# An LSTM step on one core: the forget gate in PSUM banks of its own, its product with the cell apart, and the cell by one scan

## What is computed

```python
xW = einsum('ntd,dg->ntg', x, Wx) + b
def step(carry, xw_t):
    prev_h, prev_c = carry
    a = xw_t + prev_h @ Wh                 # (2, 1024): i, f, o, g of 256 each
    i = sigmoid(a[:, :H]);  f = sigmoid(a[:, H:2*H])
    o = sigmoid(a[:, 2*H:3*H]);  g = tanh(a[:, 3*H:])
    next_c = f * prev_c + i * g
    next_h = o * tanh(next_c)
    return (next_h, next_c), next_h
x = x + lstm(x, cond)
ys = cond / sqrt(256)
d = rsqrt(einsum('bi,io->bo', ys*ys, w*w) + 1e-8)
x = x + einsum('bsi,io->bso', x * ys[:, None, :], w) * d[:, None, :]
```

## Time and profile before

| | us |
|---|---|
| median of 3 runs (lowest to highest) | 1865.49 (1864.79 to 1865.72) |
| the profiled execution | 1865.51 |
| its span, first to last instruction | 1863.7 |
| PE busy / PEld busy | 1794.8 (96%) / 1627.1 (87%) |
| DVE busy | 916.5 (49%) |
| ACT busy | 900.9 (48%) |
| POOL busy | 259.2 (14%) |
| granted TensorE clock, mean | 0.994 |

### The profile page before, as it was taken

The page is one execution under the profiler, slowest core; times in us unless marked ns, Lnnn a source line. Parts: engine busy times, 40 slices in busy tenths (PEclk is TensorE's granted clock), DMA queues, the critical chain, the costliest instruction groups (busy, mean ns, idle before and its releaser), DMA issues.

```text
span 1863.7 us, 358217 instructions
## 1 busy us (share of the span) xinstructions
PE 1794.8 (96%) x165116; PEld 1627.1 (87%) x165116; DVE 916.5 (49%) x11034; ACT 900.9 (48%) x6148; POOL 259.2 (14%) x1293
## 2 busy tenths in 40 slices
PE   7999999999999999999999999999999999999998
PEld 6888888888888888888888888888888888888886
DVE  2454544455445544454444544455444544455444
ACT  2444444444444444444444444444444444444443
POOL 0111111111111111111111111111111111111110
PEclk7999999999999999999999999999999999999999
DMA  3000000000000000000000000000000000000001
GB/s 98 0 0 0 0 0 0 0 0 0 0 0 0 0 0 0 0 0 0 0 0 0 0 0 0 0 0 0 0 0 0 0 0 0 0 0 0 0 0 45
DMA packets 4585, 6.69 MB, mean 4 GB/s; under 512 B 1248, under 2 KB 3040, under 8 KB 4576
## 3 DMA queue, kind: packets, MB, share of 16 engines
q1 hardware_dynamic: 3872, 5.51, 0.9%
q10 hardware_dynamic: 704, 1.05, 0.2%
HBM read 4.46 MB, written 2.10 MB: 4 GB/s over the span
## 4 chain that ended last, share of the span: by engine, by line
PE 85%; DVE 10%; ACT 3%; issue 2%; DMA 0%; SPq 0%; POOL 0%; DVEq 0%
PE pG L209 51%; PE pX L191 17%; PE pS L209 12%; DVE junk L340 6%; PE pF L222 3%; ACT gates L176 3%; DVE hst L351 2%; DVE pG L322 1%; PE pX L290 1%; DVE gates L340 0%; DMA xh<-in_xT_dram 0%; PE pS L281 0%; DVE ores L368 0%; SPq L105 0%; ACT tanhc L182 0%
## 5 line engine op out<-in xcount | busy, mean ns | idle before, releaser
L209 PEld LDWEIGHTS pG<-hst,wh_sb 128*32 128x32 f32 x98304 | 981.1, 111 | 219.1 <-DVE hst L351 172.1
L209 PE MATMUL pG<-hst,wh_sb 128*32 128x16 f32 x98304 | 1081.8, 186 | 60.6 <-DVE hst L351 53.4
L340 DVE CUSTOM_DVE_ANT_1 junk<-gates 128x4 f32<-128x4 f32 x4096 | 506.9, 162 | 824.7 <-ACT gates L176 772.5
L176 ACT ACTIVATE gates<-pG 128x6 f32<-128x6 f32 x2048 | 372.5, 182 | 928.7 <-PE pG L209 782.9
L209 PE MATMUL pS<-hst,wh_sb 128*32 128x16 f32 x32768 | 495.5, 185 | 0.0
L191 PE MATMUL pX<-xp,wx_sb 128*32 128x8 f32 x32896 | 459.3, 181 | 2.8 <-issue 1.8
L137 POOL TENSOR_TENSOR xh<-xh,hst 128x4 f32 (+1 forms) x1024 | 208.6, 204 | 1575.4 <-DVE hst L351 1575.4
L182 ACT ACTIVATE tanhc<-gates 128x2 f32<-128x2 f32 x2048 | 410.5, 200 | 13.5
L209 PEld LDWEIGHTS pS<-hst,wh_sb 128*32 128x32 f32 x32768 | 397.9, 108 | 0.0
L191 PEld LDWEIGHTS pX<-xp,wx_sb 128*32 128x32 f32 x32896 | 391.8, 108 | 3.2 <-issue 1.9
L351 DVE TENSOR_TENSOR hst<-tanhc,ogate 128x2 f32<-128x2 f32 x2048 | 329.7, 161 | 100.4 <-ACT tanhc L182 0.2
(11 more groups left out here) (30 smaller groups left out, 13.9 us busy)
## 6 DMA issues: line engine op xcount, KB each, us to landing
outT_dram<-ores SPq DMA_DIRECT2D x8, 256.0 KB, 2.5
xh<-in_xT_dram SPq DMA_DIRECT2D x6, 320.0 KB
wh_sb<-in_Wh_dram ACTq DMA_DIRECT2D x1, 1024.0 KB, 8.0
wx_sb<-in_Wx_dram SPq DMA_DIRECT2D x1, 1024.0 KB, 7.4
w_sb<-in_w_dram SPq DMA_DIRECT2D x1, 256.0 KB, 6.9
xh<-in_xT_dram SPq DMA_DIRECT2D x2, 64.0 KB, 7.9
condT<-in_condT_dram ACTq DMA_DIRECT2D x1, 2.0 KB, 7.7
bias_col<-in_bC_dram ACTq DMA_DIRECT2D x1, 3.0 KB, 7.4
```

What stands on the lines that cost most here:

```text
L176: act.activation(gates[:, j, :, 0:NG].rearrange("p b n -> p n b"), cells[j][:, :, cols], ACT.Sigmoid).then_inc(gates_ready[j], 1)
L209: last = pe.matmul(to[c * Q:(c + 1) * Q, :], tile(wh_sb[:, k, :], c, j, g), hst[:, k, WIDE * t:WIDE * (t + 1)], start=False, stop=True, sk ...
L340: cell = dve.tensor_tensor_reduce(out=junk[:, j, b, :], in0=gates[:, j, b, AT_I:AT_F + 1].unsqueeze(2).broadcast_to([P, 2, 2]), in1=gates[ ...
```

## The change

It does five things:

1. The forget gate's sums move from `pG` to a PSUM tensor `pH`, one bank for each half; `pX` shrinks from three banks to one. `pG` keeps i and g (`pairs`).
2. On PE the order within a step changes: behind `h_ready[0]` come 12 matmuls of half 0 and 4 of half 1 (i alone), then the wait for `h_ready[1]`; behind it the forget gate of half 0 is finished first and signals `fsum_ready[0]`, then i and g signal `sums_ready[0]`; the same for half 1.
3. ACT takes sigmoid(f) alone (`fgate`), then i and g together into `parts`, for each half. DVE multiplies f by the cell (`tensor_tensor`) and writes the product into `parts`; when both writers have signalled `parts_ready[j]`, one `tensor_tensor_scan` over 6 elements gives the cell: for each batch row s; then 1*s - 0.5; then i*(s - 0.5) + f*c. It replaces the two `tensor_tensor_reduce`.
4. On ACT the tanh of half 0 stands ahead of the output gate of half 0; for half 1 the order stays (output gate, tanh). The signal for h (`factors_ready[j]`) comes from whichever is last.
5. The carries are split (`carry_pair`, `carry_forget`, `carry_outs`), and the filler of step 3 goes.

The core of the diff:

```diff
-    FILL = (0, 0, 1, 1)
+    FILL = (0, 0, 1, 0)
...
-        pX = ctx.enter_context(nc.psum_tensor("pX", [P, K + 1, 512], F32))
+        pH = ctx.enter_context(nc.psum_tensor("pH", [P, K, 512], F32))
+        pX = ctx.enter_context(nc.psum_tensor("pX", [P, 512], F32))
...
                     for j in range(K):
+                        act.wait_ge(fsum_ready[j], it * T + (s + 1))
+                        act.activation(fgate[:, j, :], forgets[j][:, cols], ACT.Sigmoid).then_inc(fgate_ready[j], 1)
                         act.wait_ge(sums_ready[j], it * T + (s + 1))
-                        act.activation(gates[:, j, :, 0:NG].rearrange("p b n -> p n b"), cells[j][:, :, cols],
-                                       ACT.Sigmoid).then_inc(gates_ready[j], 1)
-                    for j in range(K):
+                        act.activation(parts[:, j, SCAN - 1:SCAN - 1 + 8].rearrange("p (n q) -> p n q", n=2)[:, :, ::SCAN],
+                                       pairs[j][:, :, cols], ACT.Sigmoid).then_inc(parts_ready[j], 1)
+                    def cell_tanh(j):
+                        act.wait_ge(cell_ready[j], it * T + (s + 1))
+                        return act.activation(tanhc[:, j, :], cellc[:, j, SCAN - 1::SCAN], ACT.Tanh, scale=2.0)
+
+                    def out_gate(j):
                         act.wait_ge(osum_ready[j], it * T + (s + 1))
-                        act.activation(ogate[:, j, :], outs[j][:, cols], ACT.Sigmoid)
-                        act.wait_ge(cell_ready[j], it * T + (s + 1))
-                        act.activation(tanhc[:, j, :], gates[:, j, :, AT_C], ACT.Tanh, scale=2.0).then_inc(tanh_ready[j], 1)
+                        return act.activation(ogate[:, j, :], outs[j][:, cols], ACT.Sigmoid)
+
+                    cell_tanh(0)
+                    out_gate(0).then_inc(factors_ready[0], 1)
+                    out_gate(1)
+                    cell_tanh(1).then_inc(factors_ready[1], 1)
...
                     pe.wait_ge(h_ready[0], it * T + (s + 1))
-                    for n in range(NG):
-                        cell(s, 0, n, 0)
+                    cell(s, 0, 0, 0)
+                    cell(s, 0, 2, 0)
                     if s == 0:
-                        pe.wait_ge(x_carried[1], it + 1)
+                        pe.wait_ge(forget_carried[0], it + 1)
+                    cell(s, 0, 1, 0)
+                    if s == 0:
+                        pe.wait_ge(pair_carried[1], it + 1)
                     cell(s, 1, 0, 0)
-                    cell(s, 1, 1, 0, early)
 
                     pe.wait_ge(h_ready[1], it * T + (s + 1))
-                    for n in range(NG):
-                        last = cell(s, 0, n, 1)
-                    last.then_inc(sums_ready[0], 1)
-                    cell(s, 1, 1, 0, late)
+                    cell(s, 0, 1, 1).then_inc(fsum_ready[0], 1)
+                    cell(s, 0, 0, 1)
+                    cell(s, 0, 2, 1).then_inc(sums_ready[0], 1)
                     cell(s, 1, 2, 0)
-                    for n in range(NG):
-                        last = cell(s, 1, n, 1)
-                    last.then_inc(sums_ready[1], 1)
                     if s == 0:
-                        pe.wait_ge(x_carried[K], it + 1)
+                        pe.wait_ge(forget_carried[1], it + 1)
+                    cell(s, 1, 1, 0)
+                    cell(s, 1, 1, 1).then_inc(fsum_ready[1], 1)
+                    cell(s, 1, 0, 1)
+                    cell(s, 1, 2, 1).then_inc(sums_ready[1], 1)
+                    if s == 0:
+                        pe.wait_ge(outs_carried, it + 1)
...
                     for j in range(K):
-                        dve.wait_ge(gates_ready[j], it * T + (s + 1))
-                        for b in range(B):
-                            cell = dve.tensor_tensor_reduce(
-                                out=junk[:, j, b, :], in0=gates[:, j, b, AT_I:AT_F + 1].unsqueeze(2).broadcast_to([P, 2, 2]),
-                                in1=gates[:, j, b, AT_G:AT_G + 6].rearrange("p (a c) -> p a c", a=2)[:, :, ::2],
-                                scale=1.0, scalar=0.0, op0=ALU.mult, op1=ALU.add,
-                                accum_out=gates[:, j, b, AT_C:AT_C + 1])
-                        cell.then_inc(cell_ready[j], 1)
-                        if s == T - 1 and j == 0:
-                            carry_cells(0)
+                        dve.wait_ge(fgate_ready[j], it * T + (s + 1))
+                        dve.tensor_tensor(parts[:, j, (B + 1) * SCAN - 1::SCAN], fgate[:, j, :], cellc[:, j, SCAN - 1::SCAN],
+                                          ALU.mult).then_inc(parts_ready[j], 1)
+                        if s == T - 1 and j == 1:
+                            carry_pair(0)
+                        dve.wait_ge(parts_ready[j], it * (2 * T) + 2 * (s + 1))
+                        dve.tensor_tensor_scan(cellc[:, j, :], parts[:, j, 0:B * SCAN], parts[:, j, B * SCAN:2 * B * SCAN], 0.0,
+                                               ALU.mult, ALU.add).then_inc(cell_ready[j], 1)
                     for j in range(K):
-                        dve.wait_ge(tanh_ready[j], it * T + (s + 1))
+                        dve.wait_ge(factors_ready[j], it * T + (s + 1))
...
                         if s == T - 1 and j == 0:
-                            carry_cells(1)
+                            carry_forget(0)
+                            carry_pair(1)
                     if s == T - 1:
+                        carry_forget(1)
                         carry_outs()
```

More of the change, by code:

```diff
@@ L46, in build @@
         hst = sb("hst", [P, K, T * WIDE])
-        gates = sb("gates", [P, K, B, CELL])
-        junk = sb("junk", [P, K, B, G])
+        parts = sb("parts", [P, K, 2 * B * SCAN])
+        fgate = sb("fgate", [P, K, B])
+        cellc = sb("cellc", [P, K, B * SCAN])
         ogate = sb("ogate", [P, K, B])
@@ L81, in build @@
         osum_ready = [sem(f"osum_ready{j}") for j in range(K)]
-        gates_ready = [sem(f"gates_ready{j}") for j in range(K)]
+        fsum_ready = [sem(f"fsum_ready{j}") for j in range(K)]
+        fgate_ready = [sem(f"fgate_ready{j}") for j in range(K)]
+        parts_ready = [sem(f"parts_ready{j}") for j in range(K)]
         bias_doubled = sem("bias_doubled")
-        x_carried = [sem(f"x_carried{n}") for n in range(K + 1)]
+        pair_carried = [sem(f"pair_carried{j}") for j in range(K)]
+        forget_carried = [sem(f"forget_carried{j}") for j in range(K)]
+        outs_carried = sem("outs_carried")
         cell_ready = [sem(f"cell_ready{j}") for j in range(K)]
-        tanh_ready = [sem(f"tanh_ready{j}") for j in range(K)]
+        factors_ready = [sem(f"factors_ready{j}") for j in range(K)]
         h_ready = [sem(f"h_ready{j}") for j in range(K)]
@@ L226, in _ @@
             for j in range(K):
[L227 removed]
+                clear(pG[:, j, 0:2 * WIDE])
+                clear(forgets[j])
                 clear(outs[j])
@@ L236, in _ @@
             pe.wait_ge(operands_ready, 3)
-            pe.wait_ge(x_carried[0], 1)
-            early, late = range(G // 2), range(G // 2, G)
+            pe.wait_ge(pair_carried[0], 1)
             with pe.Fori(0, NBODY) as it:
@@ L319, in _, with carry_pair, carry_forget @@
                 dve.tensor_copy(hst[:, j, h_slot(0):h_slot(0) + B], condT[:, j, :]).then_inc(h_ready[j], 1)
-            def carry_cells(j):
-                dve.tensor_tensor(cells[j][:, :, 0:ROWS], xcells[j], bias_col[:, j, :].unsqueeze(2).broadcast_to([P, NG, ROWS]),
-                                  ALU.add).then_inc(x_carried[j], 1)
+            def carry_pair(j):
+                dve.tensor_tensor(pairs[j][:, :, 0:ROWS], xcells[j][:, ::2, :], bias_col[:, j, ::2].unsqueeze(2).broadcast_to([P, 2, ROWS]),
+                                  ALU.add).then_inc(pair_carried[j], 1)
+            def carry_forget(j):
+                dve.tensor_tensor(forgets[j][:, 0:ROWS], xcells[j][:, 1, :], bias_col[:, j, 1:2].broadcast_to([P, ROWS]),
+                                  ALU.add).then_inc(forget_carried[j], 1)
             def carry_outs():
                 dve.tensor_tensor(pS[:, :, 0:ROWS], xouts, bias_o[:, :].unsqueeze(2).broadcast_to([P, K, ROWS]),
-                                  ALU.add).then_inc(x_carried[K], 1)
+                                  ALU.add).then_inc(outs_carried, 1)
             dve.wait_ge(bias_doubled, 1)
@@ L331, in _ @@
             for j in range(K):
-                carry_cells(j)
+                carry_pair(j)
+                carry_forget(j)
             carry_outs()
```

27 lines of the change are left out of this document (15 added, 12 removed).

## The result

The kernel after takes **1855.28 us** (median of 5 runs, 1853.19 to 1857.17), the one before 1865.49 (5 runs, 1864.79 to 1866.8): a ratio of 0.9944 (95% interval 0.9929 to 0.9958). It is faster, by 10.2 us. The forecast was 1831: the direction was right, but the gain was expected more than three times as large. The profiled execution took 1855.42 us, its span 1853.6.

The account below looks back on a forecast made before the run. Bound: a chain of latencies from h to h, PE waiting for h. Half 1's loop closes in 1.737 us, not 1.769: 33 us over 1020 steps, 35 with the turn; 1865.5 less 35 is 1831 us, range 1800 to 1866.

Parts of the forecast that it names:

- the rate on PE: PE's matmuls ahead of the gate sigmoids: 0.018 us a matmul, from two sigmoids 0.33 us apart, used to place the new signals.
- The chain behind the sigmoid: Half 1 on ACT and DVE: product, DVE's own signal 0.03 us, scan 0.171, tanh, h1, then 0.05 to PE.
- Rival 3: The scan on DVE is long: at 0.24 us the kernel takes 1903 us, at 0.26 1924; chance 0.12.
- Rival 4: DVE's own signal costs nothing, the scan follows the product after 0.09 us: step 1.70 us, kernel 1795 us; chance 0.04.
- The wait for h of half 1 binds: PE stops for h1 behind 16 matmuls, so half 1's slower loop sets the step at 1.737 us; chance 0.42.
- Rival 1: PE's wait for h1 does not bind, PE catches up; half 0's loop sets 1.71 us, kernel 1805 us; chance 0.22.
- Rival 2: PE's wait for h1 holds the weight load, 0.03 us: step 1.77 us at the latest, kernel 1849 to 1866; chance 0.17.
- The turn: At a body's end a stop of 0.008 us a step over 1.769 stays, less 2 us in all covered by PE's h1 wait.
- the tanh ahead: On ACT, half 0's tanh ahead of its output gate comes off that gate's way; half 0 saves 0.06 us.
- the clock at full speed in the loop without the filler: PE's clock stays full; against it rival 5, a clock fall without the filler, about 2380 us, chance 0.03.
- no carry that holds a scan: In a body's last step carries fit before half 1's scan; at worst 0.07 us there, 18 us in all; none taken.
- The filler at nothing: Dropping step 3's filler on PE changes nothing either way, since it stands where PE idles anyway.

## Why the prediction was right in direction and wrong in size

- **The failed step is the rate on PE**, "0.018 us a matmul, and I place the new signals by it". The 0.33 us between two sigmoids with 18 matmuls between them were divided by 18, and the signal between them was spread over the matmuls: it is 0.0168 a matmul and 0.025 for the signal. This held as long as the number of signals stayed; the change adds two. One of them (behind half 0's forget gate) stands between the stop for h of half 1 and half 1's forget gate. From the end of h of half 1 to that sigmoid it was 0.763, against 0.735 by the forecast's numbers: 0.028, and with 0.002 less behind the sigmoid this is the 0.026 by which the step is longer (1.763 for 1.737). The experiments show the price of a signal by adding it: +0.053 for two in the kernel before, +0.025 for one ahead of the forget gate and nothing for one behind it.
- **The 0.028 is a sum, and that one signal is nearly as large is in part luck.** Without a stop (the kernel after with ACT's old order) half 1's sigmoid(f) is 0.019 later than forecast. Three terms come to 0.022, the last an estimate: 0.025 for the new signal ahead of it; 0.014 because it leads the sigmoid of i and g by 0.159 (8 matmuls and a signal), not by 0.145; less some 0.017 that the kernel before lost and the kernel after does not. In the kernel before the signal behind the 30th matmul arrives at 0.965, where 0.782 + 10 * 0.0167 = 0.949 was due, and its matmuls ahead of the wait end on column groups 0 and 1, as in the run with the first two matmuls moved, which lost 0.017 that way. The other 0.009 lie in the stop itself.
- **The chain behind the sigmoid was right**: scan 171 ns for 171, own signal 0.035 for 0.03, h to PE 0.054 for 0.05. The forecast's terms as printed add up to 1.727, though, not to the 1.737 that it carried (h of half 1 at PE at 2.00, not 2.01); its other account, against before, gives 1.74 less 0.023, 1.717. That the carried sum fits to 0.002 is luck: the signals are each a little longer than 0.03. Rival 3 (a long scan) falls. Rival 4 (an own signal that costs nothing) falls: the scan starts 0.20 behind its product where the reduce pairs of before followed in 0.09.
- **The wait for h of half 1 binds**, by the gap and by the signals: in the kernel after, half 1's forget sums move nearly one to one with the end of h of half 1 (as that end goes from 0.473 to 0.484 behind the start of h, the signal goes from 1.213 to 1.223); with matmuls moved ahead of the wait they do not move with it. Rival 1 falls. Its number for half 0's loop without the wait, 1.71, was right: 1.763 less the stop's 0.051 is 1.712 (an estimate), and 1.754 with three matmuls moved, less their 0.050, is 1.704. The runs with that wait relieved did not reach it because the relief itself lies in half 0's way.
- **Rival 2** named a gap with a step of up to 1.77, and 1.763 lies there. Its mechanism is seen in part. Without the stop the load of the first weights behind the wait starts 0.03 ahead of its matmul; in the kernel after both start together, 0.53 behind the start of h. What it costs is at most the 0.009 above, not 0.03; no run separates it.
- **The turn**: 2 us were forecast, 8 came. The forecast read 0.008 a step over the plain 1.769 as a stop that stays at every turn. But 51 of 231 turns cost 0.12 and the rest 0.01 or less. In the kernel after none is slow, and why is open. The wait for h of half 1, a stop of 0.05, could not cover 0.12, and with the stop relieved (three or two matmuls moved) turns of 0.12 do not come back. There every turn costs some 0.033, and that cost the stop can cover in the kernel after, whose turns cost 0.001.
- **How far the direction was luck.** Plain steps gave 6 us, the turns 8, and the start and the end took 3 to 4 back. The slow turns alone, which no part of the forecast names, are some 7 us (51/231 of 256 turns by 0.12); had they stayed, the gain would be some 3 us, less than the 3.7 that the forecast called the least that tells a change from none.
- **Right as well**: the tanh ahead (its removal costs 55 us), the clock at full speed in the loop without the filler, no carry that holds a scan. The filler at nothing holds in the loop. Behind it the granted clock fell for 3.4 us in the profiled executions of the kernel after and of the kernel before without the filler of step 3; with that filler in either kernel it did not, but neither did it in the other variants that lack the filler. So the filler as cause of these 2 us is not shown.

## What to carry to other kernels

In a loop that is a chain of latencies, take PE's time apart into matmuls and signals before moving a signal: two pairs of signals with different numbers of matmuls between them give both prices. A signal that is added upstream of the value that closes the loop delays it every time, even if PE has room. And when two halves share one queue, work moved ahead of one half's wait must be priced against the other half's next need: here three matmuls relieved a stop of 0.051 and cost 0.050. Of the work that can be moved, try the part that uses other column groups than the work behind the wait begins on.

## What the runs showed of the hardware

- A completion signal in a stream of 128x32 matmuls costs 0.024 to 0.025 us. The Trainium skill ("TensorE: Matmul & The Clock Gate", section "The cost: per-tile semaphore tail") gives a tail that grows by 26.3 ns with each increment; the runs agree, and they show it within a stream, not only at its end.
- What stands close ahead of a matmul on its own column group matters. Against 0.782 and 0.0167 a matmul, half 0's forget signal (which begins on group 0) is on time with groups 2 and 3 moved ahead of it (0.815) and with groups 0 to 2 (0.832); it is 0.017 late with groups 0 and 1 (0.832) and 0.033 late with group 0 alone (0.832). So a group used one or two matmuls ago delayed it, and one used three ago did not. That it is the group's reuse that costs fits all four; only the pair with two matmuls moved compares it with nothing else changed.
- The scan of 6 elements takes 169 to 172 ns, 8 to 11 more than a plain operation on 2 (161); a DVE operation that waits for the one ahead starts 0.035 behind its end.
- An extra wait in PE's queue at the loop's turn changed the total by -7 us in one kernel and by +8 us in another. In the kernel before, PE stopped 0.12 us in the middle of its matmuls at about one turn in four, with nothing to wait for that the profile shows; with two more signals on PE, or with the new order on ACT alone, that kernel shows no such turn.
